# A routed two-layer network on one core: the sum over a token's two experts moved from DVE into adding stores

## The reference, cut to what matters

```python
x = x + conv0(_ln_c(x))
t = tokens(x);  t = t + ffn0(_ln_t(t))      # 8 experts, hidden 512, two per token
x = x + W1 @ _ln_c(x) + bias
t = tokens(x);  t = t + ffn1(_ln_t(t))      # 8 experts, hidden 1024, two per token

def ffn(xf):                                # of both layers, in short
    scores, idx = top_k(softmax(xf @ gate), 2)     # layer 0 divides the two by their sum
    return sum_k scores[k] * expert[idx[k]](xf)
```

## Time and profile before

| | us |
|---|---|
| median of 3 runs | 1334.66 |
| lowest and highest | 1327.06, 1334.68 |
| the profiled execution | 1332.33 |
| its span in the profile | 1330.6 |
| mean granted TensorE clock | 0.817 of full |

### The profile page before, as it was taken

The page is one execution under the profiler, slowest core; times in us unless marked ns, Lnnn a source line. Parts: engine busy times, 40 slices in busy tenths (PEclk is TensorE's granted clock), DMA queues, the critical chain, the costliest instruction groups (busy, mean ns, idle before and its releaser), DMA issues.

```text
span 1330.6 us, 27212 instructions
## 1 busy us (share of the span) xinstructions
PE 950.8 (71%) x7185; PEld 786.9 (59%) x7185; DVE 842.5 (63%) x1911; ACT 565.9 (43%) x1227; POOL 417.3 (31%) x479
## 2 busy tenths in 40 slices
PE   5210376837588899898870388457999999999943
PEld 4100265714567777776760268426888888888832
DVE  6999489888744555554546775683555555555545
ACT  4255422337655555555550023283443334343312
POOL 1285000001024545554540140002444434444410
PEclk8655596556789999999995695558999999999975
DMA  7066203923748778887777502104442442432258
GB/s 254 1 196 213 73 0 122 314 69 111 215 123 187 199 200 204 200 211 198 191 196 242 190 0 79 48 7 97 138 138 75 138 142 73 151 124 75 79 164 251
DMA packets 189153, 189.20 MB, mean 142 GB/s; under 512 B 91248, under 2 KB 158264, under 8 KB 188984
## 3 DMA queue, kind: packets, MB, share of 16 engines
q1 hardware_dynamic: 150600, 107.96, 29.1%
q10 hardware_dynamic: 24512, 41.95, 10.4%
q0 software_dynamic: 14000, 38.82, 10.2%
HBM read 119.46 MB, written 49.81 MB: 127 GB/s over the span
## 4 chain that ended last, share of the span: by engine, by line
PE 43%; DMA 19%; issue 15%; DVE 10%; ACT 5%; ACTq 4%; DVEq 2%; POOL 1%; SPq 1%; POOLq 1%
PE bank L699 18%; PE bank L721 14%; DMA wreg<-in_L_ffn_w_dram 9%; PE bank L632 4%; DMA xt<-region 4%; DMA region<-rows_x,fetch_now 3%; PE bank L549 2%; DMA wreg<-rows_y 2%; PE bank L604 1%; ACT wreg L821 1%; PE bank L674 1%; PE bank L757 1%; DVE region L1047 1%; DVE tok L1391 1%; ACTq L280 1%
## 5 line engine op out<-in xcount | busy, mean ns | idle before, releaser
L699 PE MATMUL bank<-xt,wreg 128*128 x3360 | 385.3, 275 | 42.9 <-DMA xt<-region 33.5
L699 PEld LDWEIGHTS bank<-xt,wreg 128*128 128x128 f16 x3360 | 328.2, 99 | 94.3 <-issue 52.8
L721 PE MATMUL bank<-wreg,region 128*128 128x256 f16 x2520 | 291.6, 273 | 9.0 <-ACT region L919 5.0
L721 PEld LDWEIGHTS bank<-wreg,region 128*128 128x128 f16 x2520 | 240.2, 98 | 50.7 <-ACT region L919 11.2
L924 ACT ACTIVATE region<-bank,b_t,wreg 128x256 f32<-128x256 f32 x280 | 142.0, 560 | 226.9 <-PE bank L699 212.5
L486 POOL DMA_INDIRECT rows_y<-region,put_now x140 | 138.5, 990 | 264.6 <-DVE region L1376 128.0
L447 POOL DMA_INDIRECT region<-rows_x,fetch_now x144 | 147.7, 1026 | 147.9 <-DMA xt<-region 77.8
L1368 DVE TENSOR_SCALAR region<-region,wreg 128x512 f16<-128x512 f32 x140 | 74.6, 533 | 72.3 <-ACT region L924 71.1
L549 PE MATMUL bank<-ident,xn 128*128 128x128 f32 x256 | 54.4, 372 | 83.6 <-DVE xn L1018 77.5
L1371 DVE SCALAR_TENSOR_TENSOR region<-region,wreg 128x512 f16<-128x512 f32 x140 | 105.9, 757 | 5.0
L1312 DVE SCALAR_TENSOR_TENSOR wreg<-wreg x70 | 49.5, 749 | 90.7 <-ACT wreg L891 70.2
(11 more groups left out here) (240 smaller groups left out, 1187.0 us busy)
## 6 DMA issues: line engine op xcount, KB each, us to landing
wreg<-in_L_ffn_w_dram SPq DMA_DIRECT2D x48, 512.0 KB, 6.0
wreg<-in_L_ffn_w_dram ACTq DMA_DIRECT2D x72, 256.0 KB
split_v<-wreg ACTq DMA_DIRECT2D x36, 512.0 KB
wreg<-in_L_ffn_w_dram SPq DMA_DIRECT2D x64, 256.0 KB, 3.1
wreg<-split_v SPq DMA_DIRECT2D x32, 512.0 KB
wreg<-rows_y SPq DMA_DIRECT2D x48, 256.0 KB, 3.6
rows_x<-region SPq DMA_DIRECT2D x16, 512.0 KB, 3.3
wreg<-in_x_dram SPq DMA_DIRECT2D x4, 1024.0 KB, 9.7
```

What stands on the lines that cost most here:

```text
L699: last = pe.matmul(to, block, x_cols[:, bass.ds(b, 1), :, xs_, k, :].rearrange("p j r n -> p (j r) n"), start=(k == 0 and ws_ + xs_ == 0), ...
L721: last = pe.matmul(yb[:, r * C:(r + 1) * C], lhs[:, c, r * P:(r + 1) * P], block, start=first, stop=end, skip_group_check=True)
```

## The change

The y table has one row per token. SP stores the residual tokens themselves into it during routing, and the two results of a token are added to that row in HBM by the store (`compute_op=ALU.add`), each already multiplied by its weight. For that each slot needs its own weight before the store, so weights travel with the gathered rows:

- `rows_x` rows have two more 32-bit words (1032 bytes), into which ACT's queue stores both weights of each token (`weights_kept`). The gather brings 1032 bytes per row.
- `moves[:, :, 1]` is taken modulo 4096; `choice` (in `region`, where the normed rows stood) tells which of the two weights a slot takes. DVE's `pick_weights` multiplies and reduces them for tile n + 1 at the end of tile n.
- Layer 0: DVE multiplies weights by the expert's factor, ACT copies y in two groups with that. Layer 1: after DVE's y, ACT multiplies `y_rows` in place, in two groups.
- `combine` and both its loops are gone. SP loads the 4 MB back into `tok` in eight DMAs (`load_tokens`); layer 0 then only has bn_stats, layer 1 PE's transposes straight from `tok`, ACT's copies, and one output store per image over four buffers.

```diff
-        rows_x = [nc.dram_tensor(f"rows_x{f}", (NT * P, 2 * C), F16, kind="Internal").ap() for f in range(2)]
+        rows_x = [nc.dram_tensor(f"rows_x{f}", (NT * P, C + 2), U32, kind="Internal").ap() for f in range(2)]
-        rows_y = [nc.dram_tensor(f"rows_y{f}", ((2 * NT + 2) * P, C), F32, kind="Internal").ap() for f in range(2)]
+        rows_y = [nc.dram_tensor(f"rows_y{f}", ((NT + 2) * P, C), F32, kind="Internal").ap() for f in range(2)]
...
 # SP, store_rows(f, i)
-                sp.dma_start(rows_x[f][bass.ds(i * 4 * P, 4 * P)].rearrange("(t p) c -> p t c", p=P),
-                             rows[:, bass.ds(4 * i, 4), :]).then_inc(rows_stored[f], 16)
+                at = bass.ds(i * 4 * P, 4 * P)
+                sp.dma_start(rows_x[f][at, 0:C].rearrange("(t p) c -> p t c", p=P),
+                             rows_bits[:, bass.ds(4 * i, 4), :]).then_inc(rows_stored[f], 16)
+                sp.dma_start(rows_y[f][at].rearrange("(t p) c -> p t c", p=P),
+                             tok[:, bass.ds(4 * i, 4), :]).then_inc(rows_stored[f], 16)
+            def store_spare(f):
+                sp.dma_start(rows_y[f][NT * P:].rearrange("(t p) c -> p t c", p=P), tok[:, 0:2, :]).then_inc(rows_stored[f], 16)
+            def load_tokens(f):
+                for i in range(HB):
+                    if i >= 4:
+                        sp.wait_ge(tok_loaded[f][i % 4], 16 + 16 * f)
+                    sp.dma_start(tok[:, 4 * i:4 * i + 4, :], rows_y[f][i * 4 * P:(i + 1) * 4 * P].rearrange("(t p) c -> p t c", p=P)
+                                 ).then_inc(tok_loaded[f][i % 4], 16)
...
 # SP, after turn_tiles(0): the wait for the stores, the tokens, then the waits for ACT's pieces, bias and layer 1's weights
+            for waited, each, more in ((y_free[0], 32, 48), (xr_loaded[0][0], 16, 48), (xr_loaded[1][0], 16, 48)):
+                with sp.Fori(even, even + 1) as m:
+                    sp.wait_ge(waited, each * m + more)
+            load_tokens(0)
...
 # POOL
-                pool.wait_ge(rows_stored[f], 16 * HB)
+                pool.wait_ge(rows_stored[f], 32 * HB + 16)
+                pool.wait_ge(weights_kept[f], 17)
...
                         nc.gpsimd.indirect_dma_start(rows_y[f], bass.IndirectOffsetOnAxis(ap=put_now[:, g_:g_ + 1], axis=0),
-                                                     y_rows[:, g_, :], None).then_inc(y_free[f], 16)
+                                                     y_rows[:, g_, :], None, compute_op=ALU.add).then_inc(y_free[f], 16)
...
                             after(n, lambda m: pool.wait_ge(xc_ready[r][f], 16 * m))
+                            after(n, lambda m: pool.wait_ge(weights_ready[f], m))
...
                 fetch_next(0, 1)
+                fetch_next(1, 0)
                 with pool.Fori(0, total // 2) as p:
                     for b in range(2):
-                        fetch_next(2 * p + b + 1, b)
                         put(2 * p + b, 2 * p + b + 1)
+                        fetch_next(2 * p + b + 2, 1 - b)
...
 # ACT, route(f)
+                act.wait_ge(weights_kept[f], 1)
+                act.dma_start(rows_x[f].rearrange("(t p) c -> p t c", p=P)[:, :, C:C + 2], tok_w.bitcast(U32)
+                              ).then_inc(weights_kept[f], 16)
...
 # ACT, experts: layer 0, then layer 1
-                            act.activation(y_rows.rearrange("p g c -> p (g c)"), yb[:], ACT.Copy, scale=fac[f][:, 2, e:e + 1]
-                                           ).then_inc(y_copied[f], 1)
+                            act.wait_ge(factors_y_ready, n + 1)
+                            for g_ in range(2):
+                                last = act.activation(y_rows[:, g_, :], yb[:, g_ * C:(g_ + 1) * C], ACT.Copy,
+                                                      scale=factors_y[:, bass.ds(n % 2, 1), g_:g_ + 1].rearrange("p a b -> p (a b)"))
+                            last.then_inc(y_copied[f], 1)
+                        else:
+                            act.wait_ge(y_half, n + 1)
+                            act.wait_ge(weights_ready[f], n + 1)
+                            for g_ in range(2):
+                                last = act.activation(y_rows[:, g_, :], y_rows[:, g_, :], ACT.Copy,
+                                                      scale=weights[:, bass.ds(n % 2, 1), g_:g_ + 1].rearrange("p a b -> p (a b)"))
+                            last.then_inc(y_copied[f], 1)
...
 # DVE, the end of route(f)
-                chain(dve.tensor_copy(moves[:, 0:GROUPS, 1], to_f))
+                dve.wait_ge(rows_stored[f], 32 * HB + 16)
+                chain(dve.memset(choice, 0.0))
+                for k, op in enumerate((ALU.is_lt, ALU.is_ge)):
+                    chain(dve.tensor_scalar(choice[:, 0:GROUPS, k], to_f, float(NT * P), None, op))
+                chain(dve.scalar_tensor_tensor(pad_f, choice[:, 0:GROUPS, 1], -float(NT * P), to_f, ALU.mult, ALU.add))
+                chain(dve.tensor_copy(moves[:, 0:GROUPS, 1], pad_f))
...
 # DVE, experts
+            def pick_weights(f, n):
+                for r in range(2):
+                    dve.wait_ge(xr_loaded[r][f], 16 * n + 16)
+                side = n if isinstance(n, int) else n % 2
+                one = lambda v: v[:, bass.ds(side, 1)]
+                dve.tensor_tensor(one(weighed), one(x_weights), choice[:, bass.ds(2 * n, 2), :].rearrange("p (j g) k -> p j g k", j=1),
+                                  ALU.mult).then_inc(weighed_ready[f], 1)
+                dve.wait_ge(weighed_ready[f], n + 1)
+                dve.tensor_reduce(one(weights), one(weighed), AX.X, ALU.add).then_inc(weights_ready[f], 1)
...
+                        else:
+                            dve.wait_ge(y_free[f], 32 * n + 16)
+                        pick_weights(f, n + 1)
                         if f == 0:
                             split_lo(n)
...
 # DVE, layer 0 after the experts (combine, combine_tiles and final_units are gone)
+            with dve.Fori(0, 2) as i:
                 for q in range(4):
+                    dve.wait_ge(tok_loaded[0][q], 16 * i + 16)
+                    for h in range(4):
+                        dve.bn_stats(st[:, bass.ds(16 * i + 4 * q + h, 1), :].rearrange("p a b -> p (a b)"),
+                                     tok[:, bass.ds(16 * i + 4 * q + h, 1), :].rearrange("p a b -> p (a b)")).then_inc(stats, 1)
```

More of the change, by code:

```diff
@@ L173, in bass_metaformer @@
         top = sb("top", [P, 4, NT])
+        tok_w = top[:, 2:4, :].rearrange("p k t -> p (k t)").rearrange("p (t k) -> p t k", k=2)
         red = sb("red", [P, 2, NT])
@@ L376, in _ @@
                     sp.wait_ge(waited, each * m + more)
-            even = total // 2 * 2
-            for waited, each in ((xr_loaded[0][0], 16), (xr_loaded[1][0], 16), (y_free[0], 32)):
-                with sp.Fori(even, even + 1) as m:
-                    sp.wait_ge(waited, each * m + 48)
             sp.dma_start(bias_rows[:], bias.rearrange("c a -> (c a)").partition_broadcast(P)).then_inc(bias_loaded, 16)
-            for i in range(HB):
-                load_outputs(0, i, i % 2)
             for e in range(2):
@@ L393, in _ @@
             sp.wait_ge(y_free[1], total // 2 * 64 + 48)
-            pairs(sp, lambda i: load_outputs(1, i))
+            load_tokens(1)
         CONSTS = 17
@@ L775, in _ @@
             experts(1, [edge(e) for e in range(E + 1)])
-            def turn_result(i):
-                for j in range(2):
-                    for h in range(UT):
-                        pe.wait_ge(y_used[2 * j + h], HB + i + 1)
-                    free(pe, fin_copied[j], i)
-                    to = turn[j][:].rearrange("p (k n) -> p k n", k=KC)
-                    for k in range(KC):
-                        for h in range(UT):
-                            last = pe.transpose(to[:, k, h * P:(h + 1) * P], xn[:, j, h, k * P:(k + 1) * P], ident[:])
-                    last.then_inc(fin_turned[j], 1)
-            pairs(pe, turn_result)
+            for u in range(NB):
+                pe.wait_ge(tok_loaded[1][u // 2 % 4], 32 + 16 * (u // 8))
+                free(pe, fin_copied, u - 1)
+                to = turn[u % 2][:].rearrange("p (k n) -> p k n", k=KC)
+                for k in range(KC):
+                    for h in range(UT):
+                        last = pe.transpose(to[:, k, h * P:(h + 1) * P], tok[:, 2 * u + h, k * P:(k + 1) * P], ident[:])
+                last.then_inc(fin_turned, 1)
         @block.scalar
@@ L960, in _ @@
             experts(1, [edge(e) for e in range(E + 1)])
[L962 to L974 removed]
+            for u in range(NB):
+                to = (xt, xn)[u % 4 // 2][:, u % 2].rearrange("p a b -> p (a b)")
+                act.wait_ge(fin_turned, u + 1)
+                free(act, fin_stored[u % 4], u // 4 * 16)
+                act.activation(to, turn[u % 2][:], ACT.Copy).then_inc(fin_copied, 1)
+                act.wait_ge(fin_copied, u + 1)
```

(14 more changed lines are left out.)

99 lines of the change are left out of this document (35 added, 64 removed).

## The result

| | before | after |
|---|---|---|
| median, both on one chip (8 runs each) | 1329.32 | 1339.82 |
| lowest and highest | 1325.54, 1334.68 | 1330.54, 1342.04 |
| ratio of after to before | | 1.0067, 95% interval 1.0042 to 1.0093 |
| span of the profiled execution | 1330.6 | 1328.7 |

The changed kernel is 0.7% slower. 1321 with a gain was forecast; the measured median lies in the range (1301 to 1362) and the direction was wrong. I read from it where the time moved, and take the sizes of the terms from ratios. I cut the timeline of both at the same instructions: the first "up" matmul of each expert loop, the last "down" matmul, the norm behind the combination.

The account below looks back on a forecast made before the run. No engine bounds the whole kernel; stages have different limits (DMA, DVE, PE). Terms 10.1 + 1.7 + 17.5 - 25.8 - 16.4 = -12.9, taken as -12 from 1332.3, gave 1320, forecast 1321; range 1301 to 1362.

Parts of the forecast that it names:

- a: First routing, layer 0: six 512 KB token stores ahead of weight loads cost 1.68 us each, +10.1 us.
- b: Before the lists: storing the weights as 4096 runs of 8 bytes on ACT's queue is covered, 0.
- c: Move lists: five chained DVE operations for one, 0.85 us more per layer, +1.7 us for both.
- d: First experts: adding stores at twice the plain DMA price, +0.5 us per tile, +17.5 us for 35 tiles.
- e: Second experts: ACT's scaling and the store pair's landing are covered by PE's 10.47 us per tile, 0.
- f: First combination: weighted adds and half the loads gone, bn_stats ends at 721.5 instead of 747.3, -25.8 us.
- g: Tail: 4.19 MB in and 4.19 MB out, some 32 us from first load to end, -16.4 us.
- cheap adding: Rival: an adding store takes no more engine time than a plain one; first experts +3, total 1304; chance 0.27.
- the DMA engines as the bound: Rival: at three times the plain price DMA work bounds the first experts, +1.6 us per tile, total 1359; chance 0.20.
- landings one behind the other: Rival: store pairs take 12 us to land, each tile in both loops some 4 longer, about 1570; chance 0.05.
- The slower side: Whole kernel: outcomes slower than 1348, from DMA-bound first experts or adding stores landing in sequence; chance 0.24.

Follow-up runs that it names:

- after_again: The changed kernel measured once more, unaltered, as the yardstick of the second group: 1.0079 of the kernel before; expert loops 345.0 and 384.1 us.
- late_tokens: The changed kernel with layer 0's token stores and the spare one behind all loads of the scan: 1.003 of the kernel before.
- load_after_landing: The changed kernel, with SP's expert weight loads in the second loop waiting until stores under way have landed: 1.0009 of the kernel before.
- two_y_buffers: The changed kernel with y alternating between two buffers and the picking of weights waiting for no landing: 1.0025 of the kernel before.
- plain_store: The changed kernel with plain stores in place of adding ones, the sum over experts left out: 0.9758 of the kernel before.
- plain_again: The changed kernel with plain stores, sum left out, measured again as the third group's yardstick: 0.9764 of the kernel before; loops 328.3 and 370.7 us.

## Why the prediction was wrong

**a** (token stores, +10.1): the mechanism held, the size was a little high: 7.75 us at the last peak. I missed that DVE isn't the only one who hands it on; the first tile also waits for PE's turning of the weights behind the lists, and it started 2.0 us later in one profile and 8.2 in another (375.7 in after_again). late_tokens puts the worth at some 5 us, loosely. **b** (8-byte runs, 0) was right: the store was issued at 285.4, landed 7.1 us later, and the first fetch is at 325.6. **c** (+1.7) was right: 8.6 us between the kernels at the move lists, of which 7.75 were there at the last peak, leave 0.8 in layer 0.

**d** (first experts, +17.5) was near in size (21.3 in the profile, 24 by ratio) and half wrong in reason. I priced an adding store in DMA time alone, twice a plain one, and that price held in this loop (2.1 to 2.2 times). But I wrote that POOL's store would still take about 0.99 us to issue. It takes 1.65 to 1.71. Imitated one by one, each of the two parts cost the loop 8 us in the profile (some 5 by the ratio). That the sum came out near is luck: 17.5 for DMA work was about twice what this work did by itself, and POOL's part wasn't there. As to the price itself, the rule of the Trainium skill that the prediction weighed (Collectives: The Full Stack, "The bandwidth ceiling: the fold count and why AG ≠ RS ≠ AR": the second read halves the rate) agrees roughly with the 2.1 to 2.2 of the first loop. It does not give the 2.9 of the second, where the measurement decides.

**e** (second experts, 0) is the step that failed: "A store pair has from 1267.2 to 1275 to land: 0." The 7.8 us, from the issue of the second store to the next y, were read off one tile in the quiet, where a plain store is followed after 2.4 us. An adding one takes 3.9 us in the quiet (1295.96 to 1299.86, below), half of that slack, and its issue begins 0.6 us later behind a longer first one; where a 2 MB weight load is issued behind it, it takes 6.8 to 10.0, and that happens at six places of this loop. Beyond the slack the wait reaches PE. I had named the rule myself, that each us without cover costs 35, and a rival for long landings, and gave it 0.05, at 12 us in every tile; it came at six tiles alone. load_after_landing and two_y_buffers show it from both sides, in one group: 383 with neither mend, 376 without the neighbour, 373 without the wait, 371 with plain stores. With 17 us (20 by the ratio) in place of 0, the forecast of -12 turns into +5 to +8, which is the sign that was measured (+10.5 between the medians).

**f** (-25.8) and **g** (-16.4) held. From the last store's issue to the end of bn_stats:

```profile
724.96 1.58 POOL L498 DMA_INDIRECT rows_y<-region,put_now  x1 [0.30 <-issue]
...
746.93 0.18 DVE L1013 TENSOR_SCALAR mean<-st_lg 128x32 f32<-128x32 f32 x1
```

22.0 us where before had 47.4 (from 700.73 to 748.1): -25.4. The tail of after:

```profile
1294.04 1.62 POOL L498 DMA_INDIRECT rows_y<-region,put_now  x1 [1.81 <-ACT region L953]
1295.96 1.58 POOL L498 DMA_INDIRECT rows_y<-region,put_now  x1 [0.30 <-issue]
...
1299.86 4.46 SPq L331 DMA_DIRECT2D tok<-rows_y  x5
...
1326.06 0.38 ACTq L990 DMA_DIRECT2D out_dram<-xn  x1
```

SP follows the last store after 3.9 us where the earlier trace rows had 2.4; from the first load to the end are 28.8 us, not 32: the reads and writes overlap better than I allowed.

Of the rivals, cheap adding fell (it is over twice a plain store), and the DMA engines as the bound fell too: with the load added the loop ran at 0.87 in 336 us, faster than with adding stores at 0.83. The third, landings one behind the other, takes -45 us for all other terms, where the prediction's own come to -29.4; by them it would have been some 1583 and not 1570. The slower side came by a mixture: all other terms made about -32 us, as plain_store shows (the prediction had -29.4), and the adding took some 41.

## What to carry to other kernels

A store that adds has three prices and not one: the time of the engine that issues it, DMA time, and a later landing. Whoever waits for its landing (a single buffer, an operand picked behind it) needs slack for the worst neighbour on the DMA engines, not for the quiet case; look for the largest transfer that can be issued just after it. Where the time of a ring is to be judged, read the loop's rare places too, since six of 35 tiles made more than half of a loss here (12 of 17 us). And an order on a queue can suit one loop and harm the next.

## What I had not expected of the hardware

An indirect store of 128 rows of 1 KB took POOL 0.99 us to issue, and 1.71 us in the mean (1.56 to 2.12) with the adding, with a small copy right behind it at 0.75 instead of 0.29 us. On the DMA engines it is split otherwise: a plain one went as 32 packets of 4096 bytes, an adding one as 128 of 1024, one per row. That is why 40 fetches and 40 adding stores count 7680 packets, where 88 plain DMAs had 4265. A packet of a quarter of the bytes took over half the time in the first loop (148 ns for 266), and 137 ns for 190 in the second, so that an adding store cost 2.1 to 2.2 times a plain one in the one and 2.9 times in the other. And its landing was 3.9 us after the start of the issue in the quiet (2.4 for plain stores, both in before and in plain_again), 10 us beside a 2 MB load.
